# Layer 1 attention of a four-layer kernel: scores of opposite partition halves by turns, exponents straight from PSUM, half of the turned probabilities copied by VectorE

## The chip, the cores and the metric

The kernel runs on one core of a Trainium2 chip. A core has TensorE (matmuls, into PSUM), VectorE, ScalarE and GpSimd, which work on SBUF; the first two of the last three also read PSUM. The metric is the device time of the one execution of the program, in microseconds (us); lower is better. The time before is 5828.37 us, the median of three runs (5816.56 to 5832.93).

## What is computed

Eight sequences of 512 tokens with 128 channels go through four layers one after the other. Layer 1 has a time-mixing branch and a branch with two sublayers (DEPTH = 2), each a local attention with 8 heads of 64 channels and then a feed-forward part. The change is in that attention:

```python
qkv = h @ wqkv                      # 128 -> 3 x 512
q = l2norm(q) * qs                  # over the 64 channels of a head
k = l2norm(k) * ksc
q, k = rotary_xpos(q, k)
o = local_attention(q, k, v)        # a token sees itself and the 64 before it
x = x + o @ wo
```

local_attention is a softmax over scores times 8, with a band mask.

## The kernel before

Everything is in fp32 and laid out with channels on partitions. A loop over the eight sequences runs four blocks, one per layer; in a block each engine has its own instruction list in program order, and semaphores tie them together. Nothing is scheduled by a planner: the order is the order of the code. Transfers play no part in layer 1.

Layer 1 runs its sublayer twice per sequence, so 16 times in the execution. A sublayer has a projection stretch and an attention stretch, then the feed-forward part.

In the projection stretch eight chunks n of 128 channels (0 to 3 are q, 4 to 7 are k, two heads each) are projected twice, plainly and with the halves of each head swapped (project). ScalarE squares the plain one, TensorE sums the squares over each head with a matmul by head64 (norms), ScalarE takes logarithm and exponential (root), giving the inverse norm. VectorE multiplies the two projections by the rotary tables (t1 and t2), GpSimd adds them, and VectorE multiplies by the inverse norm into the tile qk (turn). The time-mixing branch (time_mix) is woven in between the chunks, one step per chunk.

The attention stretch has eight units u = 2q + e: a query tile q of 128 tokens, and e says which partition half, so which head of each of the four chunk pairs, is worked on. A unit handles four heads. TensorE's list for a unit is: eight transposes of the probabilities of unit u (banks 4 and 5), the scores of unit u + 2 (four matmuls, 64 rows contracted, 192 keys), and P times V of unit u (the turned probabilities are loaded, the values with a column of ones stream, 104 columns). After each pair, turn_outputs turns the outputs through bank 4 back to channels on partitions.

VectorE's centre takes the scores out of PSUM, times 8 plus the band (two passes), reduces the maximum, and subtracts it; its outputs takes the row sum out of P·V, inverts it and scales. ScalarE's exponent is one pass over the four heads in SBUF, and it copies both banks of turned probabilities to pt, and the turned outputs to of (outputs_back). An fp32 matmul appears in the trace as two matmul records and two weight loads; a transpose as one.

Of the kernel before, what the change touches and what calls it, by code (L numbers as in the profile page):

```python
# [6 lines left out]
F32 = mybir.dt.float32  # L7
# [181 lines left out]
def build(nc, x_in, w_in, c_in, out, wcols, ccols, upto=99, probe=None):  # L189
# [5 lines left out]
    with ctx:  # L195
# [3 lines left out]
        bank = [ctx.enter_context(nc.psum_tensor(f"bank{i}", [128, 512], F32)) for i in range(8)]  # L199
# [6 lines left out]
        pick = ctx.enter_context(nc.sbuf_tensor("pick", [96, 32], BF16))  # L206
        a_neg = sb("a_neg", [128, 2 * NS])
# [22 lines left out]
        with ExitStack() as c0:  # L230
# [4 lines left out]
            with nc.Block(no_gpsimd_drain=True) as block:  # L235
# [15 lines left out]
                @block.scalar  # L251
                def _(a):
                    a.wait_ge(S["loaded"], 48)
                    act(pick[:], C("pick"), ACT.Copy)
                    act(a_neg[:], W("l2_alog"), ACT.Exp).then_inc(S["exp_a"], 1)
                    act(alpha[:, 0], W("l3_alpha"), ACT.Sigmoid).then_inc(S["alpha"], 1)
# [200 lines left out]
        def layer1():  # L457
            with ExitStack() as c:
# [14 lines left out]
                vt = sb("l1_v", [128, NT, H1 + 1, DH + 1], c)  # L473
# [3 lines left out]
                nmax = [sb(f"l1_nmax{e}", [128, 4], c) for e in range(2)]  # L477
                NU = 2 * NT
                PW = 104
                pt = [sb(f"l1_pt{i}", [128, 4, 128], c) for i in range(2)]  # L480
                oinv = sb("l1_oinv", [128, H1], c)
                ot = sb("l1_ot", [128, H1, DH], c)
# [4 lines left out]
                with nc.Block(no_gpsimd_drain=True) as block:  # L487
                    @block.tensor
                    def _(pe):
                        def score(i, u):  # L490

                            q, e = u // 2, u % 2
# [3 lines left out]
                            if u >= 2:  # L496
                                pe.wait_ge(S["scored"], 2 * (k - 1))
                            for f in range(2):
                                for s in range(2):
                                    g = 2 * f + s  # L500
                                    r = mm(bank[2 * e + f][:, 256 * s + n0:256 * s + KW],
                                           qk[64 * e:64 * e + 64, g * T + 128 * q:g * T + 128 * q + 128],
                                           qk[64 * e:64 * e + 64, (4 + g) * T + lo:(4 + g) * T + 128 * q + 128])
                                r.then_inc(S["score"], 1)

                        def attend(i, u):

                            q, e = u // 2, u % 2
                            k = NU * i + u
                            parts = (0, 1) if q else (1,)  # L510
                            pe.wait_ge(S["exp"], k + 1)
                            if k:
                                pe.wait_ge(S["pt"], 2 * k)
                            if e and q:
                                pe.wait_ge(S["of"], NT * i + q)
                            for f in range(2):
# [1392 lines left out]
```

## Time and profile before

| | before |
|---|---|
| median of three runs | 5828.37 us |
| the profiled execution, span from first to last instruction | 5822.4 us |
| TensorE matmul, weight load | 4385.6 us (75%), 2482.1 us (43%) |
| VectorE | 4514.1 us (78%) |
| ScalarE | 2924.5 us (50%) |
| GpSimd | 2325.4 us (40%) |
| mean granted TensorE clock | 0.895 |

The profiled execution gives no other time of its own than this span. The shares are averages over stages that have different limits: VectorE is the busiest overall because of layer 3, not of layer 1. So the stretches of layer 1 are read by themselves below. In the rows PE is TensorE, PEld its weight loads, DVE VectorE, ACT ScalarE, POOL GpSimd; a granted clock of 1.00 is 2.4 GHz and 0.50 is 1.2 GHz.

### The profile page before, as it was taken

Reading aid. Unit: us, or ns where it says so; the run is one execution under the profiler, and the core shown is the slowest. Engines: PE = TensorE matmul, PEld = TensorE weight load, DVE = VectorE, ACT = ScalarE, POOL = GpSimd, SP = SyncE. Lnnn points to the kernel's source line nnn. Section 1 sums busy time; section 2 is a strip of 40 time slices with the busy share of each in tenths; the row PEclk is TensorE's granted clock in tenths of the full one; section 3 lists DMA queues with packets and bytes.
Section 4 is the critical chain, followed back from the end, with each engine's and each line's share of the span. In section 5 each row is a group of like instructions: output and inputs, shape, how many; then the busy total and the mean of one; then the engine's idle time right before and its main releaser. Section 6 shows DMA issues by size and latency. Waiting matters only on the chain. (4 is left out here: it accounts for less than half of the span.)

```text
span 5822.4 us, 60164 instructions
## 1 busy us (share of the span) xinstructions
PE 4385.6 (75%) x16724; PEld 2482.1 (43%) x16724; DVE 4514.1 (78%) x8572; ACT 2924.5 (50%) x5085; POOL 2325.4 (40%) x1980
## 2 busy tenths in 40 slices
PE   5876778767787677876778767787678866788776
PEld 1533435344353443534435344353444524444344
DVE  3678966789657996579965799658995489955898
ACT  3544645446444564445644456444564445645455
POOL 0134631447204562045620456104661046610565
PEclk9998889978899888998889988998889998899888
DMA  2000000000000000000000000000000000000000
GB/s 99 1 1 2 1 3 1 1 2 1 3 1 0 2 1 3 1 1 2 1 3 1 2 1 1 3 1 2 1 1 3 1 2 1 1 3 1 2 1 2
DMA packets 3537, 22.97 MB, mean 4 GB/s; under 512 B 336, under 2 KB 336, under 8 KB 2640
## 3 DMA queue, kind: packets, MB, share of 16 engines
q1 hardware_dynamic: 3152, 18.59, 0.8%
q8 instruction: 150, 2.46, 0.2%
q14 instruction: 235, 1.93, 0.1%
HBM read 16.23 MB, written 2.36 MB: 3 GB/s over the span
## 5 line engine op out<-in xcount | busy, mean ns | idle before, releaser
L1622 POOL TENSOR_SCALAR l_pp<-l_sc,l_m 128x512 f32<-128x512 f32 x496 | 783.4, 1579 | 644.3 <-DVE l_m L1572 596.7
L1572 DVE MAX8 l_m<-l_wk 128x8 f32<-128x512 f32 x1536 | 980.6, 680 | 0.0
L224 PE MATMUL bank<-l_v,l_pt 128*128 128x99 f32 (+1 forms) x5888 | 871.4, 300 | 139.5 <-ACT l_pt L1362 114.7
L224 PEld LDWEIGHTS bank<-l_v,l_pt 128*128 128x128 f32 x5888 | 814.9, 216 | 196.7 <-ACT l_pt L1362 154.0
L1316 PE MATMUL bank<-consts,l_pp 128*128 128x128 f32 x2048 | 390.9, 323 | 526.3 <-POOL l_pp L1629 519.8
L1180 POOL TENSOR_TENSOR l_hc<-l_h,l_cn 128x1024 f32<-128x1024 f32 x128 | 302.3, 2362 | 989.0 <-DVE l_h L1130 989.0
L1316 PEld LDWEIGHTS bank<-consts,l_pp 128*128 128x128 f32 x2048 | 280.2, 165 | 959.7 <-POOL l_pp L1629 828.2
L224 PE MATMUL bank<-l_km,hold 128*128 128x512 f32 x1024 | 652.7, 727 | 43.3 <-DVE l_ol L1539 18.1
L1568 DVE MATCH_REPLACE8 l_wk<-l_m,l_wk 128x512 f32<-128x512 f32 x1024 | 684.1, 675 | 0.0
L1392 ACT ACTIVATE l_sc<-bank 128x512 f32<-128x512 f32 x512 | 303.3, 594 | 739.9 <-PE bank L224 738.5
L1629 POOL TENSOR_TENSOR l_pp<-l_pp,l_ex 128x512 f32<-128x512 f32 x496 | 631.0, 1272 | 26.4 <-ACT l_ex L1399 5.7
L865 POOL TENSOR_TENSOR l_of<-l_of,l_t 128x512 f32<-128x512 f32 x128 | 182.7, 1427 | 963.8 <-DVE l_t L796 963.8
L224 PE MATMUL bank<-hold,weights 128*128 128x512 f32 (+2 forms) x760 | 388.9, 645 | 103.4 <-issue 68.3
L1399 ACT ACTIVATE l_ex<-l_sc,l_nmx 128x512 f32<-128x512 f32 x512 | 364.4, 714 | 99.4 <-POOL l_nmx L1612 98.1
L1130 DVE TENSOR_TENSOR_SCAN l_h<-l_da,l_db 128x512 f32<-128x512 f32 x256 | 411.7, 1649 | 0.0
L1362 ACT ACTIVATE l_pt<-bank 128x512 f32<-128x512 f32 x512 | 301.4, 589 | 169.6 <-PE bank L1316 168.3
L1568 DVE MATCH_REPLACE8 l_wk<-l_m,l_sc 128x512 f32<-128x512 f32 x512 | 342.0, 675 | 0.0
L1563 DVE MAX8 l_m<-l_sc 128x8 f32<-128x512 f32 x512 | 325.8, 677 | 0.8 <-ACT l_sc L1392 0.5
L224 PE MATMUL bank<-l_hc,consts 128*128 128x512 f32 x256 | 161.9, 718 | 194.3 <-POOL l_hc L1180 194.3
L1862 POOL TENSOR_TENSOR l_sq<-l_st,hold 128x512 f32<-128x512 f32 x64 | 81.2, 1269 | 506.0 <-DVE l_st L1825 506.0
L224 PEld LDWEIGHTS bank<-hold,weights 128*128 128x128 f32 (+2 forms) x760 | 143.9, 202 | 313.2 <-issue 239.3
L224 PEld LDWEIGHTS bank<-l_km,hold 128*128 128x128 f32 x1024 | 189.6, 226 | 178.3 <-issue 120.5
(350 smaller groups left out, 8065.6 us busy)
## 6 DMA issues: line engine op xcount, KB each, us to landing
weights<-weights_dram SPq DMA_DIRECT2D x1, 11014.0 KB, 29.0
hold<-x_dram SPq DMA_DIRECT2D x9, 256.0 KB, 2.6
out_dram<-x SPq DMA_DIRECT2D x9, 256.0 KB, 3.4
consts<-consts_dram SPq DMA_DIRECT2D x1, 1503.0 KB, 32.2
rotary<-consts_dram SPq DMA_DIRECT2D x1, 1024.0 KB, 34.1
```

What stands on the lines that cost most here:

```text
L224: return nc.tensor.matmul(o, lhsT, rhs, start=start, stop=stop)
L1130: nc.vector.tensor_tensor_scan(hh[n % 2][:, k], da[n % 2][:, k], db[n % 2][:, k], 0.0, ALU.mult, ALU.add).then_inc(S["h"], 1)
L1180: nc.gpsimd.tensor_tensor(hc[n % 2][:], hh[n % 2][:], cn[n % 3][:, None, :].to_broadcast([128, 2, T]), ALU.mult).then_inc(S["hc"], 1)
L1316: r = nc.tensor.transpose(bank[3 + n % 2][:, 128 * k:128 * k + 128], pp[n % 2][:, 128 * k:128 * k + 128], C("ident"))
L1362: act(pt[n % 2][:], bank[3 + n % 2][:], ACT.Copy).then_inc(S["pt"], 1)
L1392: act(sc[n % RS][:], bank[n % 3][:], ACT.Copy).then_inc(S["sc"], 1)
L1399: act(ex[n % RM][:], sc[n % RS][:], ACT.Exp, scale=SC, bias=nmx[n % RM][:], accum_out=zs[:, q, h:h + 1]).then_inc(S["ex"], 1)
L1563: nc.vector.max(m8[n % RM][:, 0], sc[n % RS][:]).then_inc(S["top"], 1)
L1568: nc.vector.match_replace(w[:], m8[n % RM][:, k], sc[n % RS][:] if k == 0 else w[:], -3e38).then_inc(S["rest"], 1)
L1572: nc.vector.max(m8[n % RM][:, k + 1], wk_[n % 2][:]).then_inc(S["top"], 1)
L1622: nc.gpsimd.tensor_scalar(pp[n % 2][:], sc[n % RS][:], m8[n % RM][:, 3, 0:1], None, ALU.is_ge).then_inc(S["kept"], 1)
L1629: nc.gpsimd.tensor_tensor(pp[n % 2][:], pp[n % 2][:], ex[n % RM][:], ALU.mult).then_inc(S["pp"], 1)
```

## The change

A unit now is u = 2q + f, where f says which two of the four chunk pairs, so it holds four heads of both partition halves.

- Scores: the band is put into the two PSUM banks by a bf16 matmul each (eye times band), and the four score matmuls add to it, with the halves e = 0, 1 by turns. The scores of q are no longer scaled by q's inverse norm.
- q's inverse norms: the sums of squares of chunks 0 to 3 are computed by 128x2 matmuls with tokens on partitions, 32 columns in all; one small logarithm and exponential and one VectorE pass make qrs. GpSimd's sum goes straight into qk for q. Root and turn are left out for chunks 0 to 3.
- VectorE's centre is now one maximum straight from the two banks, negated, and one small product with qrs (shift).
- ScalarE's exponent reads PSUM, one instruction per head, with qrs as scale and shift as bias, and accumulates the row sum.
- VectorE inverts the row sums (share), and GpSimd multiplies the probabilities by them before they are turned.
- TensorE's list for a unit is now: scores of u + 2, transposes of u, P times V of u. P times V loads the values (64 columns) and streams the turned probabilities, into the lower and upper half of the output's partitions by turns, so outputs come out with channels on partitions: turn_outputs, and VectorE's outputs, are gone.
- ScalarE copies bank 4 of the turned probabilities, VectorE bank 5 (turn_probs).

```diff
-                            for f in range(2):
-                                for s in range(2):
+                            halves = [bank[2 * f + e].rearrange("p (s j) -> p s j", s=2)[:, :, n0:KW] for e in range(2)]
+                            for e in range(2):
+                                mm(halves[e], eye[:], band[:, None, n0:KW].to_broadcast([128, 2, KW - n0]), True, False)
+                            for s in range(2):
+                                for e in range(2):
...
+                            if u + 2 < NU:
+                                score(i, u + 2)
+                            for e in range(2):
+                                if k:
+                                    pe.wait_ge(S["pt2" if e else "pt"], k)
+                                pe.wait_ge(S["shared"], 2 * k + e + 1)
...
-                            if u + 2 < NU:
-                                score(i, u + 2)
...
+                            pe.wait_ge(S["pt"], k + 1)
+                            pe.wait_ge(S["pt2"], k + 1)
+                            for s in range(2):
+                                for d in parts:
+                                    for e in range(2):
+                                        g = 2 * f + s
+                                        r = mm(bank[6 + q % 2][64 * e:64 * e + 64, 128 * g:128 * g + 128],
+                                               vt[:, q - 1 + d, 2 * g + e], pt[e][:, 2 * s + d], d == parts[0], d == 1)
...
+                                if n < 4:
+                                    for q in range(NT):
+                                        r = mm(bank[4][:, 8 * n + 2 * q:8 * n + 2 * q + 2], sqq[n % 2][:, 128 * q:128 * q + 128],
+                                               C("head64")[:, 0:128:64])
...
+                                for e in range(2):
+                                    for s in range(2):
+                                        j = 2 * e + s
+                                        r = act(pe_[f][:, j, WIN + n0:256], bank[2 * f + e][:, 256 * s + n0:256 * s + KW],
+                                                ACT.Exp, scale=qrs[:, 2 * f + s, q, e:e + 1], bias=shift[f][:, j:j + 1],
+                                                accum_out=zs[f][:, j:j + 1])
...
+                                nc.vector.tensor_reduce(
+                                    nmax[f][:], banks[:, 2 * f:2 * f + 2].rearrange("p b (s j) -> p (b s) j", s=2)[:, :, n0:KW],
+                                    AX.X, ALU.max, negate=True).then_inc(S["max"], 1)
...
                             for u in range(NU):
+                                share(u)
                                 if u + 2 < NU:
                                     centre(u + 2)
-                                outputs(u)
+                                turn_probs(u)
...
+                            for u in range(NU):
+                                e, k, n0 = u % 2, NU * i + u, 0 if u >= 2 else WIN
+                                for f in range(2):
+                                    g.wait_ge(S["rec"], 2 * k + f + 1)
+                                    p = pe_[e][:, 2 * f:2 * f + 2, WIN + n0:256]
+                                    nc.gpsimd.tensor_tensor(p, p, rec[e][:, 2 * f:2 * f + 2, None].to_broadcast([128, 2, KW - n0]),
+                                                            ALU.mult).then_inc(S["shared"], 1)
```

TensorE's list in the middle of the attention stretch before (l_probs are the probabilities being turned, l_qk the scores, l_v and l_pt are P times V, l_ot the outputs being turned):

```order
L519 MATMUL bank<-consts,l_probs 128x128 x8
L224 MATMUL bank<-l_qk 128x192 x4
L224 MATMUL bank<-l_v,l_pt 128x104 x8
L544 MATMUL bank<-consts,l_ot 128x128 x4
L519 MATMUL bank<-consts,l_probs 128x128 x8
```

The same place of the changed kernel:

```order
L227 MATMUL bank<-band,eye 128x2x192 x2
L227 MATMUL bank<-l_qk 128x192 x4
L525 MATMUL bank<-consts,l_probs 128x128 x8
L227 MATMUL bank<-l_pt,l_v 64x128 x8
L227 MATMUL bank<-band,eye 128x2x192 x2
L227 MATMUL bank<-l_qk 128x192 x4
```

The scores moved from between transposes and P times V to ahead of the transposes, with the band ahead of them, and the output transposes are gone.

VectorE's list for one unit before, in the same stretch:

```order
L810 SCALAR_TENSOR_TENSOR l_probs<-bank,consts 128x2x192 x2
L815 TENSOR_REDUCE l_nmax<-l_probs 128x4
L817 TENSOR_TENSOR l_probs<-l_probs,l_nmax 128x4x192
L826 RECIPROCAL l_oinv<-bank 128x4
L830 TENSOR_TENSOR l_ot<-bank,l_oinv 128x4x64
```

And of the changed kernel (l_zs are the row sums, l_rec their inverses, l_pt the turned probabilities):

```order
L842 RECIPROCAL l_rec<-l_zs 128x2 x2
L828 TENSOR_REDUCE l_nmax<-bank 128x4
L832 TENSOR_TENSOR l_shift<-l_nmax,l_qrs 128x4
L850 COPY l_pt<-bank 128x2x128
L842 RECIPROCAL l_rec<-l_zs 128x2 x2
```

The copy of unit u's turned probabilities stands behind the maximum of unit u + 2, and ahead of the reciprocals of unit u + 1.

## Rows read from the trace of the kernel before

**Rows 1.** Busy time by stage: span, us busy (instructions), PEclk, DMA share, GB/s.

```profile
core 0: us, PE busy (x) PEld busy (x) DVE busy (x) ACT busy (x) POOL busy (x), PEclk, DMA share, GB/s
...
856.00:888.00 32.00, 28.36 (x65) 12.01 (x65) 21.29 (x31) 22.23 (x34) 11.19 (x8) 1.00 0.00 1
888.00:934.00 46.00, 40.73 (x268) 33.59 (x268) 26.74 (x49) 16.95 (x30) 0.00 (x0) 0.96 0.01 1
```

**Rows 2.** Timeline of two attention units: start, length, engine, line, operation, count, idle before.

```profile
909.68 1.04 PE L519 MATMUL bank<-consts,l_probs 128*128 128x128 f32 x8
...
910.32 1.08 ACT L718 ACTIVATE l_pt<-bank 128x512 f32<-128x512 f32 x2 [2.51 <-PE bank L519]
910.37 0.17 DVE L826 RECIPROCAL l_oinv<-bank 128x4 f32<-128x4 f32 x1
...
910.64 1.56 PE L224 MATMUL bank<-l_qk 64*128 64x192 f32 x8
911.29 0.84 ACT L706 ACTIVATE l_probs<-l_probs 128x768 f32<-128x768 f32 x1
...
912.14 2.03 PE L224 MATMUL bank<-l_v,l_pt 128*128 128x104 f32 x16
...
914.01 0.60 PE L544 MATMUL bank<-consts,l_ot 128*128 128x128 f32 x4
...
915.39 1.06 PE L519 MATMUL bank<-consts,l_probs 128*128 128x128 f32 x8 [0.78 <-ACT l_of L700]
```

**Rows 3.** TensorE score records: one half alone, then both halves meeting (x: in progress).

```profile
888.20:888.44 0.24, 0.24 (x4) 1.00 0.00 0
888.44:888.68 0.24, 0.24 (x7) 1.00 0.00 0
```

**Rows 4.** Timeline: values' projection, begin and end of the attention stretch.

```profile
884.20 1.88 PE L224 MATMUL bank<-weights,l_hs 128*128 128x512 f32 x4
...
887.90 2.42 PE L224 MATMUL bank<-l_qk 64*128 64x128 f32 x16 [1.82 <-DVE l_qk L781]
...
892.82 0.62 ACT L706 ACTIVATE l_probs<-l_probs 128x512 f32<-128x512 f32 x1
...
895.64 1.14 PE L224 MATMUL bank<-l_v,l_pt 128*128 128x104 f32 x8
...
928.37 2.00 PE L224 MATMUL bank<-l_v,l_pt 128*128 128x104 f32 x16 [0.34 <-ACT l_pt L718]
...
931.11 0.66 PE L544 MATMUL bank<-consts,l_ot 128*128 128x128 f32 x4 [0.73 <-DVE l_ot L830]
...
933.65 0.69 DVE L840 TENSOR_TENSOR l_x<-xn,bank 128x512 f32<-128x512 f32 x1 [2.59 <-PE bank L224]
```

**Rows 5.** Groups by line and shape: count | busy us, mean ns | idle before.

```profile
L1629 POOL TENSOR_TENSOR l_pp<-l_pp,l_ex 128x512 f32<-128x512 f32 x496 | 631.0, 1272 | 26.4 <-ACT l_ex L1399 5.7
...
L1180 POOL TENSOR_TENSOR l_hc<-l_h,l_cn 128x1024 f32<-128x1024 f32 x128 | 302.3, 2362 | 989.0 <-DVE l_h L1130 989.0
...
L1399 ACT ACTIVATION_READ_ACCUMULATOR l_ex<-l_sc,l_nmx 128x1 f32 x512 | 96.5, 189 | 0.0
L677 ACT ACTIVATE l_rn<-l_rn,consts 128x512 f32<-128x512 f32 x128 | 92.4, 722 | 4.2
L815 DVE TENSOR_REDUCE l_nmax<-l_probs 128x4 f32<-128x768 f32 x96 | 91.5, 953 | 3.3
...
L224 PE MATMUL bank<-l_parts,pick 96*128 96x512 bf16 x256 | 77.9, 385 | 24.7 <-DVE l_db L1150 14.3 <-ACT l_parts L1016 10.4
...
L410 ACT ACTIVATE L_ff<-L_ff,L_ctx,couple 128x512 f32<-128x512 f32 x24 | 19.5, 814 | 1.3
...
L1539 DVE COPY l_ol<-bank 128x288 f32<-128x288 f32 x16 | 6.4, 445 | 0.0
```

**Rows 6.** Projection stretch: a group, the nearest small matmul's group, and one wait.

```profile
L781 DVE SCALAR_TENSOR_TENSOR l_qk<-l_rn,l_of 128x512 f32<-128x512 f32 x128 | 111.3, 870 | 57.9 <-ACT l_rn L677 37.8 <-POOL l_of L865 19.7
...
L224 PE MATMUL bank<-weights,xn 128*128 128x4 f32 x64 | 11.5, 250 | 0.0
...
874.66 1.13 PE L224 MATMUL bank<-hold,weights 128*128 128x512 f32 x2 [0.81 <-DVE hold L765]
```

More of the change, by code:

```diff
@@ L198, in build @@
         c_sb = sb("consts", [128, once])
-        bank = [ctx.enter_context(nc.psum_tensor(f"bank{i}", [128, 512], F32)) for i in range(8)]
+        banks = ctx.enter_context(nc.psum_tensor("bank", [128, 8, 512], F32))
+        bank = [banks[:, i] for i in range(8)]
         x = sb("x", [128, T])
@@ L540, in turn_outputs @@
-                        def turn_outputs(i, q):
-                            pe.wait_ge(S["ot"], NU * i + 2 * q + 2)
-                            for g in range(4):
-                                r = nc.tensor.transpose(bank[4][:, 128 * g:128 * g + 128],
-                                                        ot[:, 2 * g:2 * g + 2, :].rearrange("p a d -> p (a d)"), C("ident"))
-                            r.then_inc(S["oturn"], 1)
+                            if f == 0 and q >= 2:
+                                pe.wait_ge(S["of"], NT * i + q - 1)
@@ L548, in _ @@
+                            r.then_inc(S["pv"], 1)
                         lx.pe(pe)
@@ L801, in centre @@
                             def centre(u):
-                                q, e = u // 2, u % 2
+                                q, f = u // 2, u % 2
                                 k = NU * i + u
                                 n0 = 0 if q else WIN
+                                v.wait_ge(S["score"], k + 1)
                                 if k >= 2:
-                                    v.wait_ge(S["turned"], 2 * (k - 1))
-                                for f in range(2):
-                                    v.wait_ge(S["score"], 2 * k + f + 1)
-                                    stt(pe_[e][:, 2 * f:2 * f + 2, WIN + n0:256],
-                                        bank[2 * e + f][:].rearrange("p (a j) -> p a j", a=2)[:, :, n0:KW], 8.0,
-                                        C("band")[:, None, n0:KW].to_broadcast([128, 2, KW - n0]),
-                                        ALU.mult, ALU.add).then_inc(S["scored"], 1)
@@ new lines, in share, with turn_probs @@
+                            def share(u):
+                                f, k = u % 2, NU * i + u
+                                for e in range(2):
+                                    v.wait_ge(S["exp"], 2 * k + e + 1)
+                                    if k >= 2:
+                                        v.wait_ge(S["shared"], 2 * (k - 2) + e + 1)
+                                    nc.vector.reciprocal(rec[f][:, 2 * e:2 * e + 2], zs[f][:, 2 * e:2 * e + 2]).then_inc(S["rec"], 1)
+                            def turn_probs(u):
+                                q, k = u // 2, NU * i + u
+                                v.wait_ge(S["turned"], 2 * k + 2)
+                                if k:
+                                    v.wait_ge(S["pv"], k)
+                                nc.vector.tensor_copy(pt[1][:, (0 if q else 1)::(1 if q else 2)],
+                                                      bank[5].rearrange("p (s t) -> p s t", s=4)[:, (0 if q else 1)::(1 if q else 2)]
+                                                      ).then_inc(S["pt2"], 1)
```

169 lines of the change are left out of this document (84 added, 85 removed).

## The prediction

> **What bounds the kernel now.** I read the busy time by stage first. Layer 1 runs its attention 16 times in the execution (8 sequences, 2 sublayers), and each time it takes two stretches: a projection stretch of some 31.5 us and an attention stretch of some 46 us [rows 1]. In the attention stretch TensorE is busy 40.7 of 46.0 us, VectorE 26.7, ScalarE 17.0 and GpSimd not at all; TensorE's granted clock is 0.96 there, so nearly all of it runs at the upper of its two levels (2.4 GHz). In the projection stretch TensorE is busy 28.4 of 32.0 us, with ScalarE at 22.2 and VectorE at 21.3 behind it. So TensorE ends last in both, and I go through its queue.
>
> The timeline of two units shows the cycle [rows 2]. A unit with an odd number starts its eight transposes at 909.68, its scores at 910.64, its P·V at 912.14, and the next group at 914.01: 0.96 + 1.50 + 1.87 = 4.33 us with no wait. The scores stand between the transposes and P·V, and cover the copies of the turned probabilities. After the pair comes turn_outputs (914.01), the copy of bank 4 by ScalarE, and only then the next transposes at 915.39, which need that bank (0.78 us of waiting): 1.38 us more. A pair of units thus costs 10.05 us, 5.0 per unit. The stretch starts with the first score at 887.90, waits for the first exponent (892.82) and reaches the first P·V at 895.64; the last P·V starts at 928.37, and x1 at 933.65 [rows 4]. That is 7.74 + 32.73 + 5.28 = 45.75 us.
>
> **The change, part by part.** *Opposite halves.* Before, the scores of a unit lie all in one half of the partitions. There is one place where the other half follows: the two first units' scores. In 0.24 us of the first half alone, 4 matmul records are under way; in the 0.24 us in which the two halves meet, 7 are [rows 3]. So records of opposite halves run side by side, and the queue takes the second half's records while the first half's are still waiting. From the trace: 512 columns take (1.88 - 0.16)/4 = 0.43 us per record [rows 4], 0.16 being what a row's end adds after its last record (2.03 against 1.87 [rows 2]); 192 columns then take 0.16. Eight records are 1.29 us, and the rest of the 1.50 us, 0.2 us, is what surrounds a change of the array's shape. With halves alternating I count 4 slots instead of 8: 0.65 us.
>
> *P·V* changes operands: 64 value columns are loaded and 128 columns of probabilities stream, into the lower and the upper half of the output's partitions by turns. A record takes 0.117 us now (1.87/16), whichever operand streams; no row shows two column halves side by side. Bounds: 16 slots, 1.87 us, or 8 slots, 0.90 us. I take 0.90, by the likeness to the row halves.
>
> *New on TensorE:* two bf16 matmuls that put the band into the bank. A bf16 record of 512 columns takes 0.385 us with its end [rows 5], so 0.22 without; 384 columns take 0.16, both 0.33. A unit has now four changes of shape where it had two, at 0.2 us each; the one ahead of P·V lies in a wait. Removed: the four output transposes, and the wait for bank 4.
>
> The Trainium skill (TensorEngine Tiling (Array Packing), Key Properties) says that different tiles load and multiply in parallel, and that a change of tiling mode drains TensorE. The trace agrees with the first for row halves only, and shows the second as the 0.2 us; by the page's rule alone the second would speak against this change. The skill (TensorE: Matmul & The Clock Gate, Part 3) gives 2.38 times for three column tiles; as an estimate from that page a pair would give 1.6 times, P·V 1.17 us, and the sum below would end near 5808 us.
>
> *VectorE per unit:* the two masking passes, the subtraction and the scaling of outputs go. It keeps the maximum, 0.95 us for 768 elements [rows 5], now read from two banks, two small operations, two small reciprocals (0.17 each [rows 2]), and gains a copy of 512 from PSUM: 288 took 0.445 [rows 5], so with 1.04 ns an element 0.68.
>
> *ScalarE per unit:* four exponents of 192 with scale and bias as operands, each followed by an accumulator read. The row with both operands has 0.814 for 512 [rows 5]; a plain exponent goes from 0.62 for 512 [rows 4] to 0.84 for 768 [rows 2], 0.86 ns a column, so 192 take 0.54; the read adds 0.19; two instructions in a row overlap by 0.1 (1.08 for two copies of 0.59). I get 0.53 each, 2.1 us, and with one copy and half of outputs_back 2.9 us: no bound.
>
> *GpSimd per unit:* two products of 384 elements. 512 take 1.27 and 1024 take 2.36 [rows 5], so 384 take 1.0; both 2.0 us.
>
> **The new cycle.** TensorE's order is now score(u+2), transposes(u), P·V(u): nothing covers the copies any more, and VectorE's copy stands behind the maximum of score(u+2). The loop, in order: masks 0.33, change 0.2, scores 0.65 and their end to VectorE 0.27, maximum 0.99, shift 0.1, copy 0.68, hand-over 0.06, P·V 0.90, change 0.2: 4.4 us. The transposes (0.96) run beside the maximum. A second loop is copy, reciprocals 0.2, hand-over 0.15, two products 2.0, hand-over 0.12, second half of the transposes 0.7, copy 0.7: 3.9 us, shorter. So a full unit costs 4.4 against 5.0 us.
>
> Start: the exponents of unit 0 take 1.9 instead of 0.62 us, and then masks, changes, scores of unit 2, its maximum and VectorE's copy stand ahead of the first P·V; I get 5.05 us from the first exponent where it is 2.82 now: +2.2. Middle, first to last P·V: units of 3.7, 4.0, three of 4.4, then 3.75 (no score left) and 5.6 with the first part of the output projection inside: 30.3 against 32.7, -2.4. End: P·V 1.0 shorter, and reciprocal, scaling (0.74) and output transposes (0.66) gone [rows 4]: -2.4. I add 0.5 because TensorE waits more in the first units and may sit at 1.2 GHz for a while longer. Attention stretch: -2.1 us.
>
> Projection stretch: for the four q chunks two ScalarE passes (the second is 0.72 [rows 5], the first much the same) and the last VectorE product go; that product's mean is 0.87 [rows 6], where the sum of the same shape at 933.65 takes 0.69 [rows 4]. TensorE keeps the same eight weight loads per chunk, in 128x2 matmuls; the nearest row is 0.25 for 128x4 [rows 6] with its end, so I take 0.9 per chunk for the 0.86 of now. TensorE's time does not change, but its wait of 0.81 for y [rows 6] and the ones like it hang on ScalarE work that stands behind these passes; I choose -1.1 us. If a 128x2 matmul with its two loads cost 0.25 more than I take, it is 0; if all the excess of VectorE's products were on the path too, -2.
>
> Sum: (-2.1 - 1.1) x 16 = -51 us, against 5822.4 us of span; the median stands 6 us above that, so 5777 us.
>
> **Rivals.** *The column halves of P·V don't overlap (0.20).* For it: no row shows it. P·V stays at 1.87, the loop is 5.3 us, the stretch 5.4 us longer than I forecast: +2.2 x 16 = 5864 us, slower. It decides from P·V of about 1.45 us.
>
> *GpSimd's products become the loop (0.10).* The second loop reaches 4.4 us at 1.27 us per product; its broadcast operand is not in any row. At 1.6 us the loop is 5.1, the stretch 4.5 us longer, 5849 us; in between the time is about that of before.
>
> *TensorE's clock falls in the attention stretch (0.05).* For it: TensorE waits some 1.0 us in each 4.4. Against: it waited in every second unit before, and the clock stayed. At 1.2 GHz some 2.1 us of the loop double: 16 x 8 x 2.1 gives up to 6045 us; a third of the stretch so, 5865 us. The skill (TensorE: Matmul & The Clock Gate, Part 4) says that transposes don't raise the clock; the stretch of now, with as many, has 0.96.
>
> *Nothing overlaps (0.03):* the scores too at 1.29: 5940 us. The overlap of row halves is in all 16 places of this kind, so this is nearly excluded.
>
> **How the numbers follow.** My forecast has 0.62; its own range is 5740 to 5812 us: 0.15 us per unit more or less is 18 us, the projection stretch gives 0 to -2 us each, and the page's value for P·V lies inside. 0.3% of 5828 us, about what a measurement can tell, is 17 us. Faster: nearly all of the forecast's 0.62 and a little of the GpSimd case, 0.64. Same: the rest of it and of the cases in between, 0.12. Slower: 0.24. The range 5735 to 5872 us takes in the column rival.
>
> **What the profile after would show.** P·V rows of eight slots, some 1.06 us long; if they are 2.0 us the first rival holds. VectorE's copy starting as the shift ends, and TensorE's P·V released by VectorE's copy, not by ScalarE's. GpSimd products near 1.0 us. A unit every 4.4 us. Four exponents in 2.1 us, ScalarE with idle time. The granted clock at or above 0.9 in the stretch. The projection stretch near 30.4 us. The prediction fails if P·V or a product is dearer, or if a hand-over I price at 0.1 us is several times that.

## The result and the profile after

The changed kernel takes 5721.42 us (median, 5706.05 to 5729.31) against 5822.47 us for the kernel before on the same chip: ratio 0.9826, 95% interval 0.9806 to 0.9845. That is 101 us less, where 51 had been forecast, and 14 us under the lower end of the range (5735). Run again beside the experiments, the same kernel took 5716.1 us, ratio 0.9825 [0.9809, 0.9842].

The page of the profiled execution, its totals and the granted clock of TensorE in 40 slices:

```profile
span 5720.0 us, 61822 instructions
...
PE 4228.7 (74%) x17108; PEld 2321.5 (41%) x17108; DVE 4273.7 (75%) x8380; ACT 2946.7 (52%) x5759; POOL 2505.1 (44%) x2236
...
PEclk9998989988899898988989978999889998889988
```

The same two stages as in [rows 1], for one sublayer (span, busy us by engine, clock, DMA):

```profile
840.50:870.97 30.47, 28.65 (x94) 14.64 (x96) 18.59 (x28) 17.54 (x28) 10.66 (x8) 1.00 0.00 1
870.97:911.60 40.63, 30.22 (x266) 20.59 (x262) 14.51 (x41) 23.17 (x78) 12.07 (x16) 1.00 0.00 1
```

In the attention stretch TensorE is busy 30.2 us where it was 40.7, and VectorE 14.5 where it was 26.7; GpSimd has 12.1 us of work that it did not have. TensorE now has idle time in every unit. One whole unit, in the timeline (the counterpart of [rows 2]):

```profile
890.74 1.09 PE L227 MATMUL bank<-l_pt,l_v 128*64 128x128 f32 x16 [0.93 <-DVE l_pt L850]
890.74 1.61 POOL L904 TENSOR_TENSOR l_probs<-l_probs,l_rec 128x384 f32<-128x384 f32 x2 [2.72 <-DVE l_rec L842]
...
891.76 0.50 PE L227 MATMUL bank<-band,eye 128*128 128x384 bf16 x2
...
892.19 0.92 PE L227 MATMUL bank<-l_qk 64*128 64x192 f32 x8
...
893.04 1.09 PE L525 MATMUL bank<-consts,l_probs 128*128 128x128 f32 x8
893.16 0.96 DVE L828 TENSOR_REDUCE l_nmax<-bank 128x4 f32<-128x768 f32 x1 [2.44 <-PE bank L227]
...
894.15 0.16 DVE L832 TENSOR_TENSOR l_shift<-l_nmax,l_qrs 128x4 f32<-128x4 f32 x1
...
894.23 0.69 DVE L850 COPY l_pt<-bank 128x512 f32<-128x512 f32 x1
...
895.07 1.09 PE L227 MATMUL bank<-l_pt,l_v 128*64 128x128 f32 x16 [0.93 <-DVE l_pt L850]
```

The loop can be read off the starts: P·V 890.74, band 891.76, scores 892.19, maximum 893.16, copy 894.23, P·V 895.07, that is 1.02 + 0.43 + 0.97 + 1.07 + 0.84 = 4.33 us. It is the loop that the prediction named, with VectorE's copy as the releaser of P·V, and each link is within 0.1 us of its price (1.10, 0.53, 0.92, 1.09, 0.74). The beginning and the end of the stretch, against [rows 4]:

```profile
870.66 0.72 PE L227 MATMUL bank<-l_qk 64*128 64x128 f32 x8
...
871.63 0.72 PE L227 MATMUL bank<-l_qk 64*128 64x128 f32 x8
...
872.27 1.98 PE L227 MATMUL bank<-weights,l_hs 128*128 128x512 f32 x4
...
873.43 0.60 ACT L701 ACTIVATE l_v<-bank 128x512 f32<-128x512 f32 x1 [3.07 <-PE bank L227]
873.93 0.45 ACT L721 ACTIVATE l_probs<-bank,l_shift,l_qrs 128x128 f32<-128x128 f32 x1
...
878.88 0.66 PE L227 MATMUL bank<-l_pt,l_v 128*64 128x128 f32 x8 [1.10 <-DVE l_pt L850]
...
908.29 1.09 PE L227 MATMUL bank<-l_pt,l_v 128*64 128x128 f32 x16 [0.88 <-DVE l_pt L850]
...
911.27 0.69 DVE L865 TENSOR_TENSOR l_x<-xn,bank 128x512 f32<-128x512 f32 x1 [3.12 <-PE bank L227]
```

The same instants, taken in all 16 sublayers of both traces and averaged (us per sublayer; the forecast is that of the prediction):

| part | before | after | difference | forecast |
|---|---|---|---|---|
| projection stretch | 31.44 | 30.18 | -1.26 | -1.1 |
| first score to first P·V | 7.15 | 8.40 | +1.25 | +2.2 and +0.5 |
| first to last P·V | 32.73 | 29.60 | -3.13 | -2.4 |
| last P·V to x1 | 5.28 | 2.98 | -2.30 | -2.4 |
| sum | 76.59 | 71.16 | -5.43 | -3.2 |

16 times 5.43 is 87 us. The mean of the projection stretch hides two values: in the first sublayer of each sequence it went from 31.5 to 29.8 us, in the second from 31.3 to 30.6; what makes the two differ is not shown. I also took the layers apart in the traces, each from its first instruction to the next layer's first, summed over the 8 sequences:

| kernel | span or median, us | one sublayer | layer 1 | layer 2 | layer 3 |
|---|---|---|---|---|---|
| before | span 5822.4 | 76.59 | 1515.3 | 1066.0 | 2676.5 |
| changed | span 5720.0 | 71.16 | 1429.7 | 1067.2 | 2660.7 |
| changed, again | 5716.10 | 71.11 | 1426.5 | 1064.9 | 2656.9 |
| pv_one_half | 5832.95 | 76.51 | 1519.0 | 1084.9 | 2659.2 |
| score_one_half | 5916.15 | 82.99 | 1617.6 | 1076.1 | 2670.7 |
| act_copies_both | 5726.83 | 69.80 | 1410.5 | 1084.2 | 2669.9 |
| act_both_later | 5728.32 | 69.77 | 1421.4 | 1064.9 | 2673.3 |
| later | 5753.94 | 71.04 | 1440.6 | 1072.2 | 2666.3 |
| band_in_wait | 5711.16 | 69.18 | 1405.4 | 1080.9 | 2664.3 |
| band_wait_act_both | 5685.35 | 67.62 | 1370.5 | 1076.6 | 2672.8 |
| q_passes_back | 5768.74 | 72.07 | 1452.5 | 1080.1 | 2672.9 |
| scores_back | 5840.54 | 77.57 | 1532.2 | 1077.5 | 2659.9 |
| wide_products | 5749.16 | 71.42 | 1440.1 | 1088.0 | 2653.5 |

(The layers come from the one profiled execution of each kernel, so they don't add up to the medians. The row of the kernel named later is the median of three of its four executions: the fourth took 11797 us, which nothing here explains, and isn't counted. The experiments ran on three chips, where the kernel before had 5820.48, 5824.97 and 5821.07 us.) Layer 1 explains 86 of the 102 us of span, and layer 3, whose code is the same, 16. (Layer 2 and what lies outside these three layers make up the rest; there is one trace of the kernel before.) The last two columns are the second subject of this study: they move by up to 23 us between kernels that differ in layer 1 alone.

### The profile page after: what moved, and what is told of

The parts are those of the page before. It is cut to its first block and busy times, and to the rows that moved or that the text cites. A ratio compares the mean times of both kernels' runs of the same rounds, so it can differ in the third digit from the quotient of the medians.

```text
span 5720.0 us, 61822 instructions
## 1 busy us (share of the span) xinstructions
PE 4228.7 (74%) x17108; PEld 2321.5 (41%) x17108; DVE 4273.7 (75%) x8380; ACT 2946.7 (52%) x5759; POOL 2505.1 (44%) x2236
## 5 line engine op out<-in xcount | busy, mean ns | idle before, releaser
L227 PE MATMUL bank<-l_v,l_pt 128*128 128x99 f32 x4096 | 645.6, 311 | 147.4 <-ACT l_pt L1402 131.4
L227 PEld LDWEIGHTS bank<-l_v,l_pt 128*128 128x128 f32 x4096 | 610.1, 228 | 177.7 <-ACT l_pt L1402 173.3
L1669 POOL TENSOR_TENSOR l_pp<-l_pp,l_ex 128x512 f32<-128x512 f32 x496 | 630.3, 1271 | 26.7 <-ACT l_ex L1439 4.9
L904 POOL TENSOR_TENSOR l_probs<-l_probs,l_rec 128x384 f32<-128x384 f32 (+1 forms) x256 | 193.1, 773 | 373.7 <-DVE l_rec L842 373.7
L895 POOL TENSOR_TENSOR l_qk<-l_of,l_t 128x512 f32<-128x512 f32 x64 | 81.0, 1266 | 513.9 <-DVE l_t L815 305.5
L828 DVE TENSOR_REDUCE l_nmax<-bank 128x4 f32<-128x768 f32 (+1 forms) x128 | 114.1, 891 | 224.3 <-PE bank L227 214.6
```

Source lines behind the costliest of these rows:

```text
L227: return nc.tensor.matmul(o, lhsT, rhs, start=start, stop=stop)
L1669: nc.gpsimd.tensor_tensor(pp[n % 2][:], pp[n % 2][:], ex[n % RM][:], ALU.mult).then_inc(S["pp"], 1)
```

## The experiments

**The changed kernel again**, beside the first experiments, gave the 5716.1 us told above. The question asked of it was whether layer 3's 16 us belonged to one execution alone:

> The changed kernel as it is, for the others of this chip. Layer 1 should again take some 87 us less than before. Beside layer 1 the profiled execution of the change had 16 us less in layer 3, whose code is the same. Theory A (that part is the state of TensorE's clock in that one execution): layer 3's sum over the eight sequences differs here by several us from 2660.7 us, in either direction. Theory B (the change does it): layer 3 again has about 2660 us, against 2676 before. Ratio to before 0.981 to 0.987.

Layer 1 took 89 us less than before. Layer 3 took 2656.9 us, again well under the 2676.5 of the kernel before, which speaks for theory B. How it comes about is taken up below.

**Do the halves overlap?** Two kernels send the halves' records to one half again. In pv_one_half all P·V records write the lower 64 partitions of the output (the sums over the two windows are left out, and the upper half of the outputs is not computed):

```diff
-                                        r = mm(bank[6 + q % 2][64 * e:64 * e + 64, 128 * g:128 * g + 128],
-                                               vt[:, q - 1 + d, 2 * g + e], pt[e][:, 2 * s + d], d == parts[0], d == 1)
+                                        r = mm(bank[6 + q % 2][0:64, 128 * g:128 * g + 128],
+                                               vt[:, q - 1 + d, 2 * g + e], pt[e][:, 2 * s + d])
```

> P times V writes both heads' outputs into the lower half of the output's partitions (and without accumulation over the two key parts), so the outputs are not those of the reference; the instructions are the same in number and shape. Theory A (the column halves run side by side, that is what makes the row 1.09 us): the row becomes about 1.95 us, a full unit 5.2 instead of 4.33 us, and the kernel is 5.5 to 6 us per sublayer slower than the change, 88 to 96 us, so about as slow as before. Theory B (the short row comes from loading 64 columns and not from the overlap): the row stays at 1.1 us and the time within 5 us of the change.

It took 5832.95 us, ratio to before 1.0022 [1.0011, 1.0033]. The timeline of TensorE, P·V of a full unit:

```profile
905.87 1.93 PE L227 MATMUL bank<-l_pt,l_v 128*64 128x128 f32 x16 [0.93 <-DVE l_pt L850]
```

1.93 us where it is 1.09, and the next P·V 5.17 us later where it is 4.33. Without the 0.16 us that a row's end adds, the 16 records take 0.93 us with the halves by turns and 1.77 in one half: 1.9 times, so the column halves overlap nearly fully, and this shows it by taking only that away. The Trainium skill (TensorE: Matmul & The Clock Gate, Part 3) gives 2.38 times for three column tiles, from which I had estimated 1.6 for a pair; the 1.9 measured here differs from that estimate, and the measurement decides. A sublayer grew by 5.35 us, 86 us in all, just under what was expected; the total grew by 117 against the changed kernel on the same chip, and 20 of that lie in layer 2.

In score_one_half both score records of a chunk pair read the lower 64 partitions of q and k (the upper heads' scores are not computed):

```diff
-                                    r = mm(halves[e][:, s], qk[64 * e:64 * e + 64, g * T + 128 * q:g * T + 128 * q + 128],
-                                           qk[64 * e:64 * e + 64, (4 + g) * T + lo:(4 + g) * T + 128 * q + 128], False, s == 1)
+                                    r = mm(halves[e][:, s], qk[0:64, g * T + 128 * q:g * T + 128 * q + 128],
+                                           qk[0:64, (4 + g) * T + lo:(4 + g) * T + 128 * q + 128], False, s == 1)
```

> All scores are taken from the lower partition half (both heads of a pair get the lower one's scores), so the outputs are not those of the reference; instructions and shapes are the same. Theory A (overlap of row halves gives 0.65 us per unit): the score row becomes 1.56 us instead of 0.92, a full unit 5.0 us, the kernel 4.3 to 4.8 us per sublayer slower than the change, 69 to 77 us. Theory B (the alternation gives nothing, the gain is the engines' shorter lists): the time within 5 us of the change.

It took 5916.15 us, ratio 1.0156 [1.0139, 1.0173]: 200 us over the changed kernel. The full unit is 4.97 us where the clock stays up, 0.64 us over 4.33, as expected. What was not expected is the clock. Windows of one attention stretch:

```profile
895.00:905.00 10.00, 9.37 (x36) 7.16 (x35) 2.71 (x7) 2.60 (x10) 1.61 (x2) 0.50 0.00 0
905.00:925.00 20.00, 17.32 (x103) 13.09 (x102) 5.12 (x14) 8.66 (x29) 4.83 (x6) 0.67 0.00 1
```

A clock of 0.50 is the lower of the two levels, 1.2 GHz; a full unit there takes up to 8.35 us. In 8 of the 16 sublayers, in 7 of 8 sequences, long pieces of the stretch are like this. So the rival that I had given 0.05, a clock that falls in the attention stretch, is real in a kernel that differs from this one only in which partitions the scores read.

The same run bears on the start of the stretch. From the first score to the first P·V, one sublayer of the changed kernel and one of score_one_half:

```profile
870.66:878.88 8.22, 5.53 (x37) 3.02 (x37) 3.63 (x11) 5.32 (x21) 1.22 (x2) 1.00 0.00 0
```

```profile
881.88:892.65 10.77, 9.07 (x37) 5.25 (x37) 3.63 (x11) 5.43 (x21) 1.23 (x2) 0.77 0.00 0
```

In score_one_half a stretch at 0.50 begins within 2.4 us of the first score in 13 of 16 sublayers. In the kernel before, where the scores of a unit also read one half, it is 11 of 16; in the changed kernel 2, in pv_one_half 2, and in the nine traces left, all with the halves by turns, 0 to 4. So which partitions the scores read decides most of whether the clock falls there; how it does so, no run shows.

**VectorE's copy.** In act_copies_both ScalarE makes both copies of the turned probabilities:

```diff
                                 act(pt[0][:, (0 if q else 1)::(1 if q else 2)],
                                     bank[4][:].rearrange("p (s t) -> p s t", s=4)[:, (0 if q else 1)::(1 if q else 2)],
                                     ACT.Copy).then_inc(S["pt"], 1)
+                                a.wait_ge(S["turned"], 2 * k + 2)
+                                act(pt[1][:, (0 if q else 1)::(1 if q else 2)],
+                                    bank[5][:].rearrange("p (s t) -> p s t", s=4)[:, (0 if q else 1)::(1 if q else 2)],
+                                    ACT.Copy).then_inc(S["pt2"], 1)
...
-                                turn_probs(u)
```

> ScalarE copies both banks of turned probabilities, VectorE none. Theory A (the loop is scores, maximum, copy behind it, P times V, and ScalarE has idle time): VectorE's copy is no gain; without it P times V starts 0.1 us earlier in full units and 0.4 us earlier in the first ones, 1.5 us per sublayer, 15 to 25 us faster than the change. Theory B (ScalarE is too full for a second copy): slower than the change by 0.3 us per unit, some 35 us.

A full unit takes 4.23 us, a sublayer 1.36 us less, layer 1 16 to 19 us less than in the two traces of the changed kernel: the copy behind the maximum does cost what was expected. But the whole took 5726.83 us, ratio 0.9835 [0.9819, 0.9852]: no gain, and by the medians 10 us more than the changed kernel on that chip (the single executions overlap, 5720.7 to 5728.2 against 5712.1 to 5724.8). Layer 2 gave back 17 to 19 us, layer 3 from 9 to 13.

**Where layer 2's time comes from.** The code, the data and the instruction counts of layer 2 are the same. Two of its eight passes in the trace of the changed kernel, then one of act_copies_both:

```profile
1726.50:1859.10 132.60, 97.48 (x252) 41.68 (x252) 110.14 (x123) 57.15 (x96) 66.00 (x31) 0.94 0.00 0
2432.10:2568.80 136.70, 101.89 (x252) 43.52 (x252) 109.21 (x123) 57.41 (x96) 64.34 (x32) 0.89 0.00 0
```

```profile
3141.30:3278.30 137.00, 103.56 (x252) 43.81 (x253) 109.13 (x123) 57.37 (x95) 63.53 (x32) 0.87 0.00 0
```

The same 252 matmuls are busy 97.5 us at a granted clock of 0.94 and 103.6 us at 0.87. TensorE's clock falls and rises within a pass. The theory is that where it falls depends on the moment at which the pass begins. To try that, act_both_later is act_copies_both with a delay at the end of layer 1, a product made three times in place of once:

```diff
+                        for n in range(2):
+                            tt(m[:], rs[:], h[2][:], ALU.mult).then_inc(S["late"], 1)
+                            v.wait_ge(S["late"], n + 1)
                         tt(m[:], rs[:], h[2][:], ALU.mult).then_inc(S["m"], 1)
```

> The kernel with both copies on ScalarE, and at the very end of layer 1 VectorE makes one product of 128x512 three times in place of once, so that layer 2 starts some 1.4 us later in each sequence (11 us in all). In the kernel with both copies on ScalarE layer 2, whose code is the same, took 134.3 to 137.0 us at a granted clock of 0.87 to 0.92, where the changed kernel has 132.6 at 0.94 in most sequences. Theory: the granted clock falls at places that depend on the moment at which a layer begins; 1.4 us later layer 2 begins where it begins in the changed kernel, and takes 132.6 us again, so that the kernel with more work is no slower, or up to 10 us faster (5716 to 5722 against 5727). Rival: layer 2 is slower for a reason that the delay leaves (5738 us).

It took 5728.32 us, ratio 0.9834 [0.9816, 0.9851], no slower than without the delay, though layer 1 is 10.9 us longer. Layer 2 is back at 1064.9 us from 1084.2, seven of the eight passes at 132.6 to 133.5, as these two:

```profile
1015.00:1147.60 132.60, 97.50 (x252) 41.64 (x253) 110.16 (x123) 57.06 (x95) 66.06 (x32) 0.94 0.00 0
2428.30:2560.80 132.50, 97.32 (x252) 41.55 (x252) 110.12 (x123) 57.05 (x95) 66.01 (x31) 0.94 0.00 0
```

The hoped-for few us of net gain did not come, since layer 3 took 3 us more. The counterpart, later, adds the same delay to the changed kernel:

> The changed kernel, with one VectorE product of 128x512 made three times at the end of layer 1, so that layer 2 starts 1.4 us later in each of 8 sequences; nothing else differs. By the work alone: 11 us more, all of it in layer 1. If the time of layers 2 and 3 hangs on where the low stretches of the granted clock fall in them, they change too, though their code doesn't: layer 2 would leave the 132.6 us that it has in most sequences, by up to 2 to 4 us each, as it did when layer 1 was 1.6 us shorter, and the total goes up by 20 to 35 us. If it does not hang on that, the total goes up by 11 us.

It took 5753.94 us (5744.14 to 5758.9). Layer 1 grew by 11 to 14 us, layer 2 by 5 to 7 and layer 3 by 6 to 9 over the two traces of the changed kernel. So 11 us of added work cost more than 11 us, as the theory had it: 22 to 32 us in the profiled execution, against the two of the changed kernel, and by the ratios (0.9884 [0.9865, 0.9904] against 0.9825) 34 us. In all 13 traces of this study layer 2 runs 104 times, and each pass begins in a low stretch of the clock. Three groups stand out. Where the low stretch of the clock in which a pass begins ends 3.2 to 3.8 us after the beginning (26 passes), the pass takes 132.5 to 132.9 us; at 4.2 to 4.4 us (12 passes) 136.6 to 137.3; at 4.8 to 5.1 us (19 passes) 134.3 to 135.2. The other 47 passes lie outside these groups and take 132.7 to 137.4 us, so the end of that first stretch doesn't tell the length in every case. Over all 104 the correlation between a pass's time at the low level and its length is 0.90. For layer 3 the same correlation is 0.73: a good part of its spread (327.9 to 336.6 us a pass) is of this kind, but not all of it is shown to be.

**The band.** If the loop is the serial chain read above, work that leaves it is gained in full. band_in_wait issues the band of unit u+3 between the transposes and P·V of unit u, where TensorE waits:

```diff
+                            if u < 3:
+                                put_band(i, u)
-                            for e in range(2):
-                                mm(halves[e], eye[:], band[:, None, n0:KW].to_broadcast([128, 2, KW - n0]), True, False)
...
                                 r.then_inc(S["turned"], 1)
+                            if u + 3 < NU:
+                                put_band(i, u + 3)
```

> The band matmuls of unit u+3 are issued behind the transposes of unit u, where TensorE waits for the copies, instead of ahead of the scores. Theory (the serial loop): a full unit of 4.33 us is a chain of band, change of shape, scores, maximum, copy, P·V; two band matmuls (0.50 us with their end) leave it and lie in the wait of 0.93 us ahead of P·V. A full unit then takes about 3.8 to 3.9 us, a sublayer 2.5 us less, layer 1 some 40 us less over the execution. Rival 1: the wait ahead of P·V is too short once the chain is shorter, or the bank of unit u+3 is not yet free there (it waits for the exponents of unit u+1), so that TensorE stands in front of P·V: a unit stays near 4.3 us. Rival 2: the gain in layer 1 is there, but the unchanged layers 2 and 3 take another time, as they did with both copies on ScalarE (+17 us in layer 2, +10 in layer 3), so that the total shows less.

It took 5711.16 us, ratio 0.9802 [0.9786, 0.9819]. TensorE's timeline:

```profile
892.87 1.09 PE L227 MATMUL bank<-l_pt,l_v 128*64 128x128 f32 x16 [0.61 <-DVE l_pt L861]
893.89 0.92 PE L227 MATMUL bank<-l_qk 64*128 64x192 f32 x8
894.74 1.09 PE L534 MATMUL bank<-consts,l_probs 128*128 128x128 f32 x8
895.67 0.49 PE L227 MATMUL bank<-band,eye 128*128 128x384 bf16 x2
896.77 1.09 PE L227 MATMUL bank<-l_pt,l_v 128*64 128x128 f32 x16 [0.61 <-DVE l_pt L861]
```

A full unit takes 3.90 us: exactly the link of 0.43 is gone, and a sublayer is 2.0 us shorter, where I had put in 2.5: five units gain 0.43 each instead of 0.5, the one without scores gains nothing, and the start is 0.08 us longer. The theory of the loop holds. The sublayers gained 32 us and the total shows 13, by the two ratios, which was the second rival: layer 2 took 14 to 16 us more, and layer 3 4 to 7. band_wait_act_both makes both edits.

> Both edits: the band matmuls in the wait, and both turned copies by ScalarE. If the loop is serial and the copy behind the maximum costs what the run with both copies on ScalarE showed (0.1 us per full unit, 1.2 us per sublayer), a unit takes 3.6 to 3.8 us, a sublayer 3.5 to 4 us less than in the changed kernel, layer 1 55 to 65 us less. If another loop (transposes, copy, P·V, exponents, reciprocal, product) becomes the bound at 3.9 us, as I worked out for the changed kernel, there is nothing beyond the run with the band in the wait alone.

It took 5685.35 us, ratio 0.9760 [0.9744, 0.9777]. It beats both kernels: 3.80 us per full unit, 3.5 us less per sublayer, layer 1 56 to 59 us less than in the two traces of the changed kernel, of which layers 2 and 3 gave back 22 to 28. The second loop, which I had at 3.9 us, did not stop it.

**The projection stretch.** q_passes_back puts the two ScalarE passes for each q chunk back, with a result that nobody reads:

```diff
+                                if n < 4:
+                                    a.wait_ge(S["ss"], 8 * i + n + 1)
+                                    act(rn[n % 2][:], sqq[n % 2][:], ACT.Ln, scale=NORM_SCALE,
+                                        bias=C("floor")).then_inc(S["extra"], 1)
+                                    a.wait_ge(S["extra"], 4 * i + n + 1)
+                                    act(rn[n % 2][:], rn[n % 2][:], ACT.Exp, scale=-0.5, bias=C("norm_back")).then_inc(S["extra2"], 1)
```

> The two ScalarE passes over 512 columns for each of the four q chunks are put back as passes whose result nobody reads; VectorE's product for q stays away, and all of the attention stretch is as changed. If the projection stretch's 1.26 us (31.44 to 30.18) come from the ScalarE passes alone, it goes back to 31.4 us and the kernel is 20 us slower than the changed one; if they come from VectorE's product, it stays at 30.2 us; if both are needed, in between.

5768.74 us, ratio 0.9906 [0.9889, 0.9922]. The projection stretch went from 30.18 to 31.45 us, where it was before the change (31.44):

```profile
846.18:877.63 31.45, 28.64 (x90) 14.32 (x90) 18.94 (x27) 22.54 (x35) 10.18 (x8) 1.00 0.00 1
```

So the gain is not there without taking the ScalarE passes away; with them back, the absence of VectorE's product for q gives nothing. Whether it would have cost something to leave that product in while the passes go was not run. The kernel as a whole is some 46 us slower than the changed one by the two ratios, where 20 was expected; the sublayers are 15 of it, and layers 2 and 3 some 25 to 31 in the profile.

**The order in the queues.** scores_back undoes one part of the change, in two queues at once: TensorE has transposes, scores, P·V again, and VectorE copies ahead of the maximum.

```diff
-                            if u + 2 < NU:
-                                score(i, u + 2)
                             for e in range(2):
...
                                 r.then_inc(S["turned"], 1)
+                            if u + 2 < NU:
+                                score(i, u + 2)
...
+                                turn_probs(u)
                                 if u + 2 < NU:
                                     centre(u + 2)
-                                turn_probs(u)
```

> One part undone: TensorE's queue has transposes, scores of unit u+2, P·V again, as in the kernel before, and VectorE makes its copy ahead of the maximum. Everything else is as changed. The copies now lie beside the scores (the wait of 0.93 us ahead of P·V goes), but the reciprocals of unit u+1 stand behind the maximum of unit u+2 in VectorE's queue, and the products and the next transposes behind them. Theory (queues in series): the loop is transposes 1.1, change and band 0.5, scores 0.92, maximum 1.1, reciprocal 0.2, products 0.8 and their hand-over: 4.9 to 5.0 us per full unit instead of 4.33, a sublayer some 4 us longer, 65 to 75 us in all (5785). Rival (TensorE's own time decides): its records add up to 3.2 us, the wait ahead of P·V is hidden, and a unit takes 3.4 us, a sublayer 4 us less (5655).

5840.54 us, ratio 1.0041 [1.0026, 1.0056]: with everything else of the change in place, the old order loses all of the gain. The timeline shows the chain:

```profile
904.90 1.09 PE L227 MATMUL bank<-l_pt,l_v 128*64 128x128 f32 x16
905.01 0.96 DVE L828 TENSOR_REDUCE l_nmax<-bank 128x4 f32<-128x768 f32 x1 [0.49 <-PE bank L227]
...
906.09 0.27 DVE L842 RECIPROCAL l_rec<-l_zs 128x2 f32<-128x2 f32 x2
...
906.33 1.61 POOL L904 TENSOR_TENSOR l_probs<-l_probs,l_rec 128x384 f32<-128x384 f32 x2 [3.31 <-DVE l_rec L842]
...
907.30 0.63 PE L523 MATMUL bank<-consts,l_probs 128*128 128x128 f32 x4 [1.31 <-POOL l_probs L904]
```

P·V no longer waits, but the next transposes wait 1.31 us for GpSimd's product, which waited for a reciprocal, which stood behind the maximum. A full unit takes 4.93 us, within the 4.9 to 5.0 of the theory. The total is 55 us more than it said; the sublayer is 6.4 us longer instead of 4, and the granted clock around the stretch is 0.86 to 0.97 where the changed kernel has 1.00 in 13 of 16: here the clock falls too. Put together from the shortest start (7.76 us) and the shortest of each unit (4.14, four of 4.92, 4.70, 5.62), the part from the first score to the last P·V would take 41.9 us against 37.6, 4.3 longer, as the theory said; the other 2.1 us come with the lower clock.

**GpSimd's slack.** wide_products has the products take 256 columns of each row:

```diff
-                                    p = pe_[e][:, 2 * f:2 * f + 2, WIN + n0:256]
+                                    p = pe_[e][:, 2 * f:2 * f + 2, 0:256]
```

> GpSimd's products take all 256 columns of each probability row instead of the 192 that are used (the other 64 are zeros): 512 elements per instruction where it was 384, in the first two units 512 where it was 256. By the measured 0.81 us for 384 an instruction takes 1.07 us, below the 1.27 us from which I put the second loop at 4.4 us. Theory: the loop over the products has slack, full units stay at 4.33 us, only the short units ahead and behind grow, 0.5 us per sublayer, 8 us in all. Rival: the products are in the loop already, and a full unit grows by two times 0.26 us, 16 x 3 x 0.5 us, 25 us and more.

5749.16 us, ratio 0.9871 [0.9855, 0.9888]. In the timeline:

```profile
892.46 1.09 PE L227 MATMUL bank<-l_pt,l_v 128*64 128x128 f32 x16 [0.93 <-DVE l_pt L850]
892.47 2.04 POOL L904 TENSOR_TENSOR l_probs<-l_probs,l_rec 128x512 f32<-128x512 f32 x2 [2.29 <-DVE l_rec L842]
...
896.80 1.09 PE L227 MATMUL bank<-l_pt,l_v 128*64 128x128 f32 x16 [0.93 <-DVE l_pt L850]
```

1.04 us an instruction where 384 elements take 0.83, and P·V still every 4.33 us: the products have slack in the full units, as the prediction's second loop said. Only the last unit but one, which has no scores, follows them, from 3.26 to 3.69 us. That is 7 us in all, near the 8 expected. By the two ratios the total rose by 27 us, and again it is layer 2, 1088.0 us, with five passes at 137 us.

## Why the prediction was wrong, step by step

The mechanism was right: halves side by side, TensorE's loop through VectorE's copy, ScalarE and GpSimd with time to spare. No rival held in this kernel. The size was off by half, in these terms.

- **The clock, forecast +0.5 us per sublayer, was -0.8.** This is the step that failed. I took the start of the stretch, 7.74 us, from one sublayer [rows 4], and added 0.5 for waits that might keep TensorE at 1.2 GHz. But the low clock was in the kernel before. In windows of that very start, and in the timeline of another sublayer of the kernel before (x16 are its scores, x4 the values' projection):

```profile
887.90:889.40 1.50, 1.50 (x13) 1.50 (x14) 0.52 (x2) 0.00 (x0) 0.00 (x0) 0.77 0.00 0
889.40:892.20 2.80, 2.80 (x8) 1.54 (x7) 2.70 (x6) 0.00 (x0) 0.00 (x0) 0.51 0.00 0
```

```profile
980.61 1.71 PE L224 MATMUL bank<-l_qk 64*128 64x128 f32 x16 [1.61 <-DVE l_qk L781]
982.25 1.99 PE L224 MATMUL bank<-weights,l_hs 128*128 128x512 f32 x4
```

  The scores took 2.42 us in [rows 4] and take 1.71 here. 11 of the 16 starts before had such a low stretch and were 7.2 to 7.8 us long; the other five were 6.1 to 6.2. After the change 14 of 16 are 8.22 or 8.23 us, 13 of them with no low clock at all, and two, with such a stretch, 9.6 and 9.7. At the same clock the change adds 8.22 - 6.15 = 2.1 us, which is the forecast's +2.2; on the mean it adds 1.25. The wait that I feared (TensorE waits more in the first units) did not bring the clock down; the scores by turns took the low stretch out of most starts, as score_one_half shows.
- **Middle, forecast -2.4, measured -3.1.** Full units 4.33 for 4.4 (three of them, 0.2), the first two 3.63 and 3.90 for 3.7 and 4.0 (0.2), and the unit without scores 3.26 for 3.75 (0.5). The last hangs on GpSimd, as wide_products shows, and I had its product at 1.0 us from instructions with other operands [rows 5]; it is 0.83, two of them 0.35 us less. These make 0.9; the mean gains 0.7, since in one sublayer the low clock stretched the first two units to 5.15 and 5.47 us.
- **End, forecast -2.4, measured -2.30. Projection, forecast -1.1, measured -1.26**: right, though I had read one of the two kinds of sublayer, and the gain goes when ScalarE's passes come back, which q_passes_back shows. The forecast's upper end for that term, -2 with all the excess of VectorE's products on the path too, was not reached.
- **P·V at 0.90 us, chosen without a row:** 0.93. Scores and the change after them, 0.65 + 0.2: 0.85 (892.19 to 893.04). The band, 0.53 with its change: 0.43. VectorE's copy 0.68: 0.69. An exponent 0.53: 0.49 to 0.50 from one to the next.
- **Unchanged layers, forecast 0, measured -16 us**, all in layer 3. The prediction had no term for them. For layer 2 the experiments show that its time depends on when it begins, through the clock; that layer 3's 16 us have this cause is likely by the correlation and by its spread between kernels (2653.5 to 2676.5 us), but no run isolates it.

Together: 16 x 2.2 = 36 us from the terms of the sublayer, of which 21 are the clock at the start and 12 the middle, and 16 us from layer 3, make the some 51 us that the forecast was short in the span.

## What to carry to other kernels

Read a stage at several of its repetitions, with the granted clock beside each, before taking a duration from one: a start of 7.74 us was 6.15 us of work and 1.6 us of low clock. When several engines share a loop, price the chain link by link and then each queue's order; moving 0.43 us of TensorE work into a wait was worth exactly 0.43 us per unit, and putting one matmul group and one VectorE copy back in their old places cost the whole gain, a third of it through the clock. And where a kernel's unchanged stages move by 10 to 20 us through the clock, judge an edit by its own stage as well as by the total: a gain of 1.4 us per sublayer did not show in the total at all.

## What the runs showed of the hardware

- Two column halves of TensorE's array work side by side: 16 records of 128 columns by turns in 0.93 us, in one half in 1.77.
- The same 252 matmuls of layer 2 are busy 97.5 to 103.6 us, and the layer takes 132.5 to 137.3 us, by where the stretches at the lower clock fall in it; a delay of 1.4 us ahead of it moved its sum over 8 passes from 1084 to 1065 us in one kernel and from 1065 or 1067 to 1072 in another.
- Scores that read one half of the partitions instead of both by turns brought long stretches at a clock of 0.50, though TensorE had no more idle time in a unit (0.93 us before P·V in one, 0.92 in the other). P·V in one half did not: its stretches stayed near 1.00. At the start of the attention stretch a low stretch begins in 13 and 11 of 16 sublayers in the traces of the two kernels whose scores read one half of the partitions, and in 0 to 4 of 16 in the eleven traces with the halves by turns. What makes the difference stays open.
- GpSimd's product with a broadcast operand takes 0.61, 0.83 and 1.04 us for 256, 384 and 512 elements a partition.
